# A graph-transformer layer: q and feed-forward matmuls ahead of the values in plain-block steps, two pairs of heads side by side

## The chip, the core and the metric

One core of one Trainium2 chip runs the whole program: TensorE (PE) for matmuls, VectorE (DVE), ScalarE (ACT) and GpSimd (POOL) for the rest, SyncE (SP) for issuing DMAs. The metric is device time of one execution in microseconds (us), and lower is better.

## The reference, cut to what matters

```
qkv = layer_norm(x, g1, be1) @ w_qkv            # x: 4096 x 128, 8 heads of 16
scores = einsum('nhd,mhd->hnm', q, k) * SCALE
scores = where(adj != 0, scores, -inf)          # adj: 4096 x 4096, int32
attn = softmax(scores, axis=-1)
out = einsum('hnm,mhd->nhd', attn, v).reshape(n, 128)
x = x + out @ w_proj + b_proj
h2 = layer_norm(x, g2, be2)
return x + gelu(h2 @ w1 + b1) @ w2 + b2         # hidden width 512
```

## The kernel before, in words

A prologue makes keys, values and masks for all 4096 rows. Then the queries go by in eight tiles of 512. A tile has 64 steps: four pairs of heads, 16 steps for each, and each step takes two blocks of 128 keys (`BLOCKS`). The code of an iteration `i` does tile `i` and also finishes tile `i - 1`; flags b, c, d say which of these parts exist (next tile to prepare, this tile, tile before). In the text, "step 23" is the iteration's step `g = 23`, and TensorE's instructions of step 23 are those that its loop `body` writes for that g. Behind tile 7 one more iteration, the drain, only finishes the last tile.

Each engine has an order that is written out by hand, and semaphores connect them. In one step:
- TensorE makes two row-score units into `ring_ps` (`row`, L960: scores with queries on the partitions, from which VectorE takes the masked row maximum, L763, for a pair that comes later), then the mask matmuls (L1112) and the score matmuls (L1127) of two blocks into `score_ps`, then two more row units, then the values: `weigh_values` (L1023) multiplies the probabilities of the step three steps back (`LAG`) by v and adds into `pv_ps`. Behind the values comes what the tables `ACT_FILLS` and `DVE_FILLS` give for the step.
- ScalarE takes the exponential of both blocks (L728), two of them in each step, then the fill of `ACT_FILLS`.
- VectorE takes four row maxima, then the fill of `DVE_FILLS`.
- GpSimd multiplies by the mask those blocks that have no mask matmuls ("plain" blocks, one in each odd step; `mask_probs`, L517), converts the adjacency for the next tile (L452, L456), splits maxima, adds q parts (L595), and does gelu's polynomial and gate (`bend`, `gate`) and the second layer norm's apply.

`score_ps` has two halves that are used in turn. `score_turn` makes TensorE wait, before it writes place n, until ScalarE has taken place n - 2. A fill of `ACT_FILLS` has a place of its own behind the two of its step, so it waits for the first exponential of its own step; the second block of the next step waits for ScalarE to have taken the fill. In an odd step the plain block comes first: its scores, then the masks and scores of the other block. In an even step both mask groups come first, then both scores; with a fill ahead, the second of these mask groups (x4 of the x8) is the one that waits.

Fills of `ACT_FILLS`: h2 transposed (`h2t`, steps 16, 17), the layer up (`up`, L1046, steps 19, 21, 23, 25; ScalarE takes it twice, L689 and L690), q of the next tile (`q`, L1036, steps 31, 34, 37, 41; ScalarE takes it twice, L675 and L676), and the shifts (`shift`, L927, two short copies L612 on ScalarE, steps 4, 14, 20, 30, 36, 46, 52, 62). Fills of `DVE_FILLS`: for each pair the softmax sums (`sums`, L1056) in the step four behind the pair's end and the way back of the reciprocals (`back`, L1062) one later, the projection of the tile before (`proj`, L1071, steps 6 and 7), the layer down (`down`, steps 30 to 33).

When a pair's 16 steps are through, `pv_ps` holds it in four groups of 32 rows: two heads, for each of the two blocks of a step. ScalarE copies it out in one piece (`take_values`, L701, 128x512) at the start of step 3, 19, 35 or 51, ahead of that step's exponentials. TensorE's values of that step start the next pair and wait for the copy. `sums` adds both parts of a head by a matmul with `sum_sel`, `back` spreads the reciprocals, VectorE multiplies (L863), and `proj` adds four pairs.

## Time and profile before

| | |
|---|---|
| runs | 1806.6, 1814.01 and 1814.49 us, median 1814.01 |
| the profiled execution | 1812.5 us, of which 1810.7 us are its span, 1.8 us lie around it |
| busy share | TensorE 92%, VectorE 78%, ScalarE 72%, GpSimd 65% |
| chain that ended last | TensorE 71%, ScalarE 15%, issue 10%, VectorE 2% |
| first and last copy of a pair (L701) | start at 180.1 and 1764.0 us |

The table is read against the span: a share of 92% for TensorE is an average over a short prologue, eight tiles that are alike and the drain. The chain says which engine the end hung on, step by step. What a change in one step is worth has to be read in that step, where TensorE and ScalarE take turns in waiting.

### The profile page before, as it was taken

Reading aid. Unit: us, or ns where it says so; the run is one execution under the profiler, and the core shown is the slowest. Engines: PE = TensorE matmul, PEld = TensorE weight load, DVE = VectorE, ACT = ScalarE, POOL = GpSimd, SP = SyncE. Lnnn points to the kernel's source line nnn. Section 1 sums busy time; section 2 is a strip of 40 time slices with the busy share of each in tenths; the row PEclk is TensorE's granted clock in tenths of the full one; section 3 lists DMA queues with packets and bytes.
Section 4 is the critical chain, followed back from the end, with each engine's and each line's share of the span. In section 5 each row is a group of like instructions: output and inputs, shape, how many; then the busy total and the mean of one; then the engine's idle time right before and its main releaser. Section 6 shows DMA issues by size and latency. Waiting matters only on the chain.

```text
span 1810.7 us, 48122 instructions
## 1 busy us (share of the span) xinstructions
PE 1673.6 (92%) x17826; PEld 553.9 (31%) x17826; DVE 1421.2 (78%) x4495; ACT 1300.8 (72%) x1443; POOL 1179.4 (65%) x1113
## 2 busy tenths in 40 slices
PE   6989999999999999999999999999999999999985
PEld 3422222323223232323223232323223232233223
DVE  6888889877898779887888779887898778987601
ACT  4547777677776777777776877677776877777771
POOL 5944586568855787468855688458865688457441
PEclk9869999999999999999999999999999999999996
DMA  7710035202450035301360035300351024500000
GB/s 214 168 42 2 25 108 110 54 1 66 135 100 2 13 106 117 66 1 54 114 133 2 1 100 124 77 2 26 123 106 47 2 77 124 77 2 1 8 7 6
DMA packets 168846, 115.24 MB, mean 64 GB/s; under 512 B 139298, under 2 KB 149156, under 8 KB 168612
## 3 DMA queue, kind: packets, MB, share of 16 engines
q1 hardware_dynamic: 157860, 103.78, 23.7%
q10 hardware_dynamic: 10752, 8.39, 1.6%
q8 instruction: 141, 2.31, 0.5%
q14 instruction: 93, 0.76, 0.1%
HBM read 74.39 MB, written 4.19 MB: 43 GB/s over the span
## 4 chain that ended last, share of the span: by engine, by line
PE 71%; ACT 15%; issue 10%; DVE 2%; DMA 1%; POOL 0%; SPq 0%; ACTq 0%; DVEq 0%; POOLq 0%
PE pv_ps L1023 19%; PE ring_ps L960 14%; PE score_ps L1127 12%; PE score_ps L1112 12%; ACT probs L728 12%; PE score_ps L1046 2%; PE ring_ps L1080 2%; PE ring_ps L1071 2%; PE ring_ps L1056 2%; PE ring_ps L1062 2%; PE score_ps L1036 2%; PE score_ps L984 2%; ACT q_stack L612 1%; ACT hidden L689 1%; DMA adj_in<-adj 1%
## 5 line engine op out<-in xcount | busy, mean ns | idle before, releaser
L763 DVE CUSTOM_DVE_ANT_0 masked_out<-ring_ps,row_mask 128x512 bf16<-128x512 f32 x2048 | 1310.3, 687 | 163.2 <-PE ring_ps L960 129.4
L728 ACT ACTIVATE probs<-score_ps,score_scale 128x1024 f32<-128x1024 f32 x1024 | 1089.0, 1113 | 358.0 <-PE score_ps L1127 350.4
L517 POOL TENSOR_TENSOR probs<-probs,keep 128x1024 int32<-128x1024 int32 x256 | 604.4, 2362 | 324.3 <-ACT probs L728 313.3
L1023 PE MATMUL pv_ps<-probs,v_ones 128*17 128x512 f32 x4096 | 539.2, 599 | 0.5 <-POOL probs L517 0.4
L960 PE MATMUL ring_ps<-k_stack,q_stack 51*64 51x512 f16 x4096 | 493.3, 397 | 13.3 <-DVE row_max L763 12.8
L1127 PE MATMUL score_ps<-q_stack,k_stack 51*64 51x512 f16 x4096 | 373.5, 391 | 26.6 <-ACT probs L728 7.4
L1112 PE MATMUL score_ps<-mask_t,ident_bf 64*64 64x512 bf16 x3072 | 276.1, 387 | 60.9 <-ACT probs L728 14.6
L960 PEld LDWEIGHTS ring_ps<-k_stack,q_stack 51*64 51x64 f16 x4096 | 165.8, 104 | 454.7 <-DVE row_max L763 401.9
L1127 PEld LDWEIGHTS score_ps<-q_stack,k_stack 51*64 51x64 f16 x4096 | 116.9, 104 | 229.2 <-PE score_ps L1112 181.1
L763 DVE DVE_READ_ACCUMULATOR2_ANT row_max<- 128x1 f32 x2048 | 169.4, 83 | 0.0
L1112 PEld LDWEIGHTS score_ps<-mask_t,ident_bf 64*64 64x64 bf16 x3072 | 92.4, 105 | 211.3 <-ACT probs L728 114.1
L456 POOL TENSOR_SCALAR row_mask<-row_mask 128x1024 bf16<-128x1024 bf16 x124 | 129.9, 1047 | 23.9 <-POOL row_mask L452 20.2
L452 POOL TENSOR_SCALAR row_mask<-adj_in 128x1024 bf16<-128x1024 uint32 x124 | 129.2, 1042 | 3.6 <-DVE row_max L763 1.7
L1023 PEld LDWEIGHTS pv_ps<-probs,v_ones 128*17 128x17 f32 x4096 | 68.1, 95 | 141.5 <-issue 110.1
L461 POOL TENSOR_SCALAR max_unit<-neg_max 128x4 f32<-128x4 f32 x64 | 12.7, 199 | 84.2 <-DVE neg_max L773 82.5
L860 DVE RECIPROCAL recip<-ring_ps 128x8 f32<-128x8 f32 x32 | 6.6, 208 | 77.5 <-PE ring_ps L1056 77.5
L612 ACT COPY q_stack<-score_ps 2x256 f16<-2x256 f16 x128 | 46.6, 364 | 9.5 <-PE score_ps L927 7.2
L876 DVE TENSOR_TENSOR rows<-ring_ps,x_res 128x128 f32<-128x128 f32 x32 | 9.3, 292 | 54.5 <-PE ring_ps L1080 54.5
L863 DVE TENSOR_TENSOR attn<-ring_ps,attn 128x512 f32<-128x512 f32 x32 | 22.1, 692 | 37.3 <-PE ring_ps L1062 37.3
L509 POOL TENSOR_SCALAR keep<-mask_t 128x512 int32<-128x512 bf16 x64 | 39.8, 622 | 5.4
L1046 PE MATMUL score_ps<-h2T,w_sb 128*128 128x512 f32 x64 | 39.8, 707 | 3.0 <-ACT hidden L693 2.3
L1080 PE MATMUL ring_ps<-w_sb,hidden 128*128 128x128 f32 x256 | 38.2, 295 | 2.0 <-DVE rows L876 1.1
(106 smaller groups left out, 969.6 us busy)
## 6 DMA issues: line engine op xcount, KB each, us to landing
adj_in<-adj SPq DMA_DIRECT2D x128, 512.0 KB, 4.1
xnT_dram<-attn ACTq DMA_DIRECT2D x8, 256.0 KB, 3.9
mask_t<-row_mask SPq DMA_TRANSPOSE x128, 3.4
xq<-xnT_dram ACTq DMA_DIRECT2D x8, 256.0 KB, 2.6
x_res<-x ACTq DMA_DIRECT2D x8, 256.0 KB, 4.4
out<-rows ACTq DMA_DIRECT2D x8, 256.0 KB, 2.6
w_sb<-L_gnn_w SPq DMA_DIRECT2D x2, 256.0 KB
probs<-x SPq DMA_DIRECT2D x1, 256.0 KB, 2.9
```

Source lines behind the costliest of these rows:

```text
L452: nc.gpsimd.tensor_scalar(target, adj_in[:, half, :].bitcast(U32), 1.0, 0.0, ALU.min, ALU.max)\
L456: nc.gpsimd.tensor_scalar(target, target, BIG, -BIG, ALU.mult, ALU.add).then_inc(mask_done, 1)
L517: nc.gpsimd.tensor_tensor(view, view, keep[:, KEPT.index(m), :].unsqueeze(1).broadcast_to([128, 2, TILE]), ALU.mult).then_inc(probs_masked, 1)
L612: last = nc.scalar.copy(stack[r:r + SHIFT_PARTS, p, 256 * jj:256 * (jj + 1)], bank.bitcast(F16)[r:r + SHIFT_PARTS, 0:256])
L728: nc.scalar.activation(probs[:, (2 * g + n) % SLOTS, :], score_ps[:, half:half + 2, :].rearrange("p a n -> p (a n)"), ACT.Exp, scale=score ...
L763: nc.vector.tensor_tensor_reduce(out=masked_out[:, place % 3, :], in0=ring_ps[:, place % 3, :], in1=row_mask[:, j, ch * 512:(ch + 1) * 512 ...
L960: last = nc.tensor.matmul(ring_ps[64 * t:64 * (t + 1), place % 3, :], stack[rows, p, first:first + 64], k_stack[rows, p, ch, K_FIRST:], st ...
L1023: last = nc.tensor.matmul(pv_ps[32 * k:32 * k + HD + 1, :], v_ones[:, block_of(g, b), 2 * p + a, :], probs[:, (2 * g + b) % SLOTS, a * TIL ...
L1046: last = nc.tensor.matmul(bank, w1_sb[:, 128 * f:128 * (f + 1)], h2T[:, :], start=True, stop=True)
L1080: last = nc.tensor.matmul(bank[:, 0:128], hidden[:, f, 128 * s:128 * (s + 1)], w2_sb[:, f, :], start=(f == 0), stop=(f == FC - 1))
L1112: last = nc.tensor.matmul(bank[to, :], ident_bf[keys, keys], mask_t[keys, source, :], start=True, stop=False)
L1127: last = nc.tensor.matmul(bank[64 * t:64 * (t + 1), :], k_stack[rows, p, m // 4, at + 64 * t:at + 64 * (t + 1)], q_stack[par][rows, p, :], ...
```

## The change

The fills of the odd steps of `ACT_FILLS` (h2t 1, the four `up`, the `q`) come ahead of the values on TensorE; the q of step 34 goes to step 35, so that all q stand in odd steps. ScalarE now copies a finished pair in two pieces of 64 rows into a new tile `halves`, on the partitions that its pair has there (even pair below, odd pair above). Behind every second pair GpSimd adds the two parts (`sum_values`, 128x512) into `attn`, in which two pairs now lie side by side, four heads in groups of 32 rows. So there are two `sums` and two ways back for a tile in place of four (steps 4 and 36), the way back of the tile before is split over steps 5 and 6, and the projection has half the matmuls and goes to steps 7 and 8. TensorE's values wait for the copy pieces (`values_taken`), its sums for GpSimd's add (`attn_ready`). The copy no longer waits for the projection. The projection's padded weights come by one small DMA less.

```diff
-ACT_FILLS = {16: ("h2t", 0), 17: ("h2t", 1), 31: ("q", 0), 34: ("q", 1), 37: ("q", 2), 41: ("q", 3)}
+ACT_FILLS = {16: ("h2t", 0), 17: ("h2t", 1), 31: ("q", 0), 35: ("q", 1), 37: ("q", 2), 41: ("q", 3)}
...
-DVE_FILLS = {4: ("sums", PAIRS - 1), 5: ("back", PAIRS - 1), 6: ("proj", 0), 7: ("proj", 1)}
+DVE_FILLS = {4: ("sums", FOURS - 1), 5: ("back", FOURS - 1, 0, 2), 6: ("back", FOURS - 1, 2, 4),
+             7: ("proj", 0), 8: ("proj", 1)}
...
-for _p in range(PAIRS - 1):
-    DVE_FILLS.update({QUARTER * (_p + 1) + 4: ("sums", _p), QUARTER * (_p + 1) + 5: ("back", _p)})
+DVE_FILLS.update({2 * QUARTER + 4: ("sums", 0), 2 * QUARTER + 5: ("back", 0, 0, SUB)})
...
+            def sum_values(n, f):
+
+                pool.wait_ge(values_taken, n)
+                settled(pool)
+                nc.gpsimd.tensor_tensor(attn[:, f, :], halves[:, 0, :], halves[:, 1, :], ALU.add).then_inc(attn_ready, 1)
...
+                    if d and g == LAG + 1:
+                        sum_values(i * PAIRS, FOURS - 1)
+                    if c and g == 2 * QUARTER + LAG + 1:
+                        sum_values(i * PAIRS + 2, 0)
...
-            def take_values(i, p, seen, proj):
+            def take_values(n, p, seen):
 
                 act.wait_ge(pv_done, seen)
-                if proj is not None:
-                    act.wait_ge(row_full, proj)
-                nc.scalar.copy(attn[:, p, :], pv_ps[:, :]).then_inc(attn_ready, 1)
+                if n >= 2:
+                    act.wait_ge(attn_ready, n // 2)
+                own = slice(64 * (p % 2), 64 * (p % 2 + 1))
+                nc.scalar.copy(halves[own, 0, :], pv_ps[0:64, :])
+                nc.scalar.copy(halves[own, 1, :], pv_ps[64:128, :]).then_inc(values_taken, 1)
...
-                    pe.wait_ge(attn_ready, i * PAIRS + p)
+                    pe.wait_ge(values_taken, i * PAIRS + p)
...
-                    for s in range(SUB):
+                    if what[2] == 0:
+                        pe.wait_ge(row_taken, made(ROWS, i, bcd, DVE_PLACE[g - 1]))
+                    for s in range(what[2], what[3]):
...
-                        for p in range(PAIRS):
-                            last = nc.tensor.matmul(bank[:, 128 * t:128 * (t + 1)], attn[:, p, 128 * s:128 * (s + 1)],
-                                                    wp_pad[:, p, :], start=(p == 0), stop=(p == PAIRS - 1))
+                        for f in range(FOURS):
+                            last = nc.tensor.matmul(bank[:, 128 * t:128 * (t + 1)], attn[:, f, 128 * s:128 * (s + 1)],
+                                                    wp_pad[:, f, :], start=(f == 0), stop=(f == FOURS - 1))
...
+                    if g in act_fills and g % 2 == 1:
+                        act_fill(i, bcd, g, act_fills[g])
                     if g < LAG and d:
                         weigh_values(i - 1, made_by(i - 1), STEPS - LAG + g)
                     if g >= LAG and c:
                         weigh_values(i, bcd, g - LAG)
-                    if g in act_fills:
+                    if g in act_fills and g % 2 == 0:
                         act_fill(i, bcd, g, act_fills[g])
```

TensorE in tile 3, step 23 and the start of step 24, before (`ring_ps` are rows, `mask_t` masks, `q_stack1,k_stack` into `score_ps` scores, `pv_ps` the values, `h2T,w1_sb` the layer up):

```order
L960 MATMUL ring_ps<-k_stack,q_stack1 64x512 x4
L1127 MATMUL score_ps<-q_stack1,k_stack 64x512 x4
L1112 MATMUL score_ps<-mask_t,ident_bf 64x512 x4
L1127 MATMUL score_ps<-q_stack1,k_stack 64x512 x4
L960 MATMUL ring_ps<-k_stack,q_stack1 64x512 x4
L1023 MATMUL pv_ps<-probs,v_ones 17x512 x4
L1046 MATMUL score_ps<-h2T,w1_sb 128x512
L960 MATMUL ring_ps<-k_stack,q_stack1 64x512 x4
L1112 MATMUL score_ps<-mask_t,ident_bf 64x512 x8
```

and after:

```order
L971 MATMUL ring_ps<-k_stack,q_stack1 64x512 x4
L1138 MATMUL score_ps<-q_stack1,k_stack 64x512 x4
L1123 MATMUL score_ps<-mask_t,ident_bf 64x512 x4
L1138 MATMUL score_ps<-q_stack1,k_stack 64x512 x4
L971 MATMUL ring_ps<-k_stack,q_stack1 64x512 x4
L1057 MATMUL score_ps<-h2T,w1_sb 128x512
L1034 MATMUL pv_ps<-probs,v_ones 17x512 x4
L971 MATMUL ring_ps<-k_stack,q_stack1 64x512 x4
L1123 MATMUL score_ps<-mask_t,ident_bf 64x512 x8
```

The layer up has moved ahead of the values; nothing else has.

TensorE in tile 3, from the values of step 5 to the fill of step 6 and the rows behind it, before (`ident,recip` the way back, `wp_pad,attn` the projection):

```order
L1023 MATMUL pv_ps<-probs,v_ones 17x512 x4
L1062 MATMUL ring_ps<-ident,recip 32x128 x16
L960 MATMUL ring_ps<-k_stack,q_stack1 64x512 x4
L1112 MATMUL score_ps<-mask_t,ident_bf 64x512 x8
L1127 MATMUL score_ps<-q_stack1,k_stack 64x512 x8
L960 MATMUL ring_ps<-k_stack,q_stack1 64x512 x4
L1023 MATMUL pv_ps<-probs,v_ones 17x512 x4
L1071 MATMUL ring_ps<-wp_pad,attn 128x128 x8
L960 MATMUL ring_ps<-k_stack,q_stack1 64x512 x4
```

and after:

```order
L1034 MATMUL pv_ps<-probs,v_ones 17x512 x4
L1074 MATMUL ring_ps<-ident,recip 32x128 x8
L971 MATMUL ring_ps<-k_stack,q_stack1 64x512 x4
L1123 MATMUL score_ps<-mask_t,ident_bf 64x512 x8
L1138 MATMUL score_ps<-q_stack1,k_stack 64x512 x8
L971 MATMUL ring_ps<-k_stack,q_stack1 64x512 x4
L1034 MATMUL pv_ps<-probs,v_ones 17x512 x4
L1074 MATMUL ring_ps<-ident,recip 32x128 x8
L971 MATMUL ring_ps<-k_stack,q_stack1 64x512 x4
```

The way back stands in two pieces of 8, the second where the first projection was; that one now stands in step 7, with 4 matmuls for 8.

ScalarE in tile 3 around the copy of step 35, before (`q_neg` and `q_x` are the two takes of a q fill):

```order
L675 ACTIVATE q_neg<-score_ps,part_coef 128x512
L676 COPY q_x<-score_ps 128x512
L739 DMA out<-rows2 128x4x128
L701 COPY attn<-pv_ps 128x512
L728 ACTIVATE probs<-score_ps,score_scale 128x1024 x4
L612 COPY q_stack1<-score_ps 2x256 x2
L728 ACTIVATE probs<-score_ps,score_scale 128x1024 x2
L675 ACTIVATE q_neg<-score_ps,part_coef 128x512
```

and after:

```order
L738 ACTIVATE probs<-score_ps,score_scale 128x1024 x6
L749 DMA out<-rows2 128x4x128
L713 COPY halves<-pv_ps 64x512
L714 COPY halves<-pv_ps 64x512
L738 ACTIVATE probs<-score_ps,score_scale 128x1024 x2
L686 ACTIVATE q_neg<-score_ps,part_coef 128x512
L687 COPY q_x<-score_ps 128x512
L738 ACTIVATE probs<-score_ps,score_scale 128x1024 x2
```

The copy is two pieces, and the take of the second q has gone from ahead of the copy to behind the exponentials of step 35.

## Rows read from the trace of the kernel before

**Rows 1.** The page: span, and busy time of each engine.

```profile
span 1810.7 us, 48122 instructions
...
PE 1673.6 (92%) x17826; PEld 553.9 (31%) x17826; DVE 1421.2 (78%) x4495; ACT 1300.8 (72%) x1443; POOL 1179.4 (65%) x1113
```

**Rows 2.** One line, the copy of a finished pair: shortest/median/longest, first and last start.

```profile
L701 ACT COPY attn<-pv_ps x32: 584/586/599, 180.1 to 1764.0; 128x512 f32<-128x512 f32 x32
```

**Rows 3.** Timeline of TensorE, tile 3, steps 22 to 24: start, us, instruction [idle before].

```profile
807.38 0.63 PE L1127 MATMUL score_ps<-q_stack,k_stack 51*64 51x512 f16 x8
...
811.16 1.05 PE L1023 MATMUL pv_ps<-probs,v_ones 128*17 128x512 f32 x8
812.14 1.12 PE L1046 MATMUL score_ps<-h2T,w_sb 128*128 128x512 f32 x2
...
814.63 0.41 PE L1112 MATMUL score_ps<-mask_t,ident_bf 64*64 64x512 bf16 x4 [0.80 <-ACT q_x L690]
814.87 0.65 PE L1127 MATMUL score_ps<-q_stack,k_stack 51*64 51x512 f16 x8
```

**Rows 4.** Timeline of ScalarE over the same steps.

```profile
807.90 2.12 ACT L728 ACTIVATE probs<-score_ps,score_scale 128x1024 f32<-128x1024 f32 x2 [0.35 <-PE score_ps L1127]
810.22 2.12 ACT L728 ACTIVATE probs<-score_ps,score_scale 128x1024 f32<-128x1024 f32 x2 [0.20 <-PE score_ps L1127]
813.31 0.69 ACT L689 ACTIVATE hidden<-score_ps,b_col 128x512 f32<-128x512 f32 x1 [0.96 <-PE score_ps L1046]
813.89 0.68 ACT L690 ACTIVATE q_x<-score_ps,b_col 128x512 f32<-128x512 f32 x1
```

**Rows 5.** Timeline of ScalarE, steps 34 and 35: exponentials, the copy of a pair.

```profile
849.68 2.12 ACT L728 ACTIVATE probs<-score_ps,score_scale 128x1024 f32<-128x1024 f32 x2 [2.12 <-PE score_ps L1127]
...
853.33 0.60 ACT L701 COPY attn<-pv_ps 128x512 f32<-128x512 f32 x1
853.81 2.14 ACT L728 ACTIVATE probs<-score_ps,score_scale 128x1024 f32<-128x1024 f32 x2
```

**Rows 6.** A group of short copies: busy us, mean ns, idle before.

```profile
L612 ACT COPY q_stack<-score_ps 2x256 f16<-2x256 f16 x128 | 46.6, 364 | 9.5 <-PE score_ps L927 7.2
```

**Rows 7.** Timeline of TensorE, tile 3, steps 52 and 53.

```profile
907.66 1.05 PE L1056 MATMUL ring_ps<-sum_sel,attn 128*128 128x2 f32 x8
...
909.10 0.39 PE L1112 MATMUL score_ps<-mask_t,ident_bf 64*64 64x512 bf16 x4
...
911.19 1.06 PE L1062 MATMUL ring_ps<-ident,recip 128*32 128x128 f32 x32
```

**Rows 8.** Timeline of ScalarE, step 52.

```profile
908.27 0.74 ACT L612 COPY q_stack<-score_ps 2x256 f16<-2x256 f16 x2
```

**Rows 9.** Timeline of TensorE, step 6: a projection.

```profile
753.89 2.05 PE L1071 MATMUL ring_ps<-wp_pad,attn 128*128 128x128 f32 x16
```

**Rows 10.** Timeline of TensorE, steps 31, 36 and 42.

```profile
838.00 1.05 PE L1023 MATMUL pv_ps<-probs,v_ones 128*17 128x512 f32 x8
...
856.25 0.64 PE L1127 MATMUL score_ps<-q_stack,k_stack 51*64 51x512 f16 x8
...
877.29 0.41 PE L1112 MATMUL score_ps<-mask_t,ident_bf 64*64 64x512 bf16 x4 [0.69 <-ACT q_x L676]
```

**Rows 11.** Timeline of ScalarE, step 31.

```profile
837.07 2.12 ACT L728 ACTIVATE probs<-score_ps,score_scale 128x1024 f32<-128x1024 f32 x2 [0.47 <-PE score_ps L1127]
```

**Rows 12.** Timeline of GpSimd, tile 3, the masks of step 25 and what precedes them.

```profile
822.19 0.62 POOL L526 TENSOR_SCALAR rows<-rows 128x512 f32<-128x512 f32 x1 [0.97 <-ACT rows L690]
822.99 1.27 POOL L529 TENSOR_TENSOR rows<-rows,hidden 128x512 f32<-128x512 f32 x1 [0.18 <-POOL rows L526]
...
826.27 2.37 POOL L517 TENSOR_TENSOR probs<-probs,keep 128x1024 int32<-128x1024 int32 x1
```

**Rows 13.** Timeline of TensorE, step 28.

```profile
828.71 1.05 PE L1023 MATMUL pv_ps<-probs,v_ones 128*17 128x512 f32 x8
```

**Rows 14.** Timeline of TensorE, the drain behind tile 7.

```profile
1768.36 3.75 PE L1071 MATMUL ring_ps<-wp_pad,attn 128*128 128x128 f32 x16 [0.88 <-DVE attn L863]
```

More of the change, by code:

```diff
@@ L32 @@
 PAIRS = HEADS // 2
+FOURS = PAIRS // 2
 HALF = 64
@@ L96, in made_for @@
         return "b"
-    if what[0] == "shift" or (what[0] in ("sums", "back") and what[1] < PAIRS - 1):
+    if what[0] == "shift" or (what[0] in ("sums", "back") and what[1] < FOURS - 1):
         return "c"
@@ L277, in program @@
         max_part = sb("max_part", [128, 2, 4, SHIFT_PARTS], F16)
-        attn = sb("attn", [128, PAIRS, TILE], F32)
-        recip = sb("recip", [128, SUB, 2], F32)
+        attn = sb("attn", [128, FOURS, TILE], F32)
+        halves = sb("halves", [128, BLOCKS, TILE], F32)
+        recip = sb("recip", [128, SUB, 4], F32)
         x_res = sb("x_res", [128, SUB, DIM], F32)
@@ L298, in program @@
         xn_rows = [rows2[:, :, :], x_res[:, :, :]]
-        xnT = [attn[:, p, :] for p in range(4)]
+        xnT = [attn[:, 0, :], attn[:, 1, :], halves[:, 0, :], halves[:, 1, :]]
         item_neg = [hidden[:, n // 2, 256 * (n % 2):256 * (n % 2) + 256].bitcast(F16) for n in range(DEPTH)]
@@ L859, in take_fill @@
                 if what[0] == "sums":
-                    nc.vector.reciprocal(recip[:, :, :], bank[:, 0:2 * SUB].rearrange("p (s a) -> p s a", a=2))\
+                    nc.vector.reciprocal(recip[:, :, :], bank[:, 0:4 * SUB].rearrange("p (s k) -> p s k", k=4))\
                       .then_inc(row_taken, 1)
                 elif what[0] == "back":
-                    nc.vector.tensor_tensor(attn[:, what[1], :], bank, attn[:, what[1], :], ALU.mult)\
+                    own = slice(128 * what[2], 128 * what[3])
+                    nc.vector.tensor_tensor(attn[:, what[1], own], bank[:, own], attn[:, what[1], own], ALU.mult)\
                       .then_inc(row_taken, 1)
@@ L1158, in constants @@
 def constants():
-    c = np.zeros((128, 134), np.float32)
+    c = np.zeros((128, 136), np.float32)
     c[:, 0:128] = np.eye(128)
-    for a in range(2):
-        for b in range(BLOCKS):
-            c[64 * b + 32 * a + HD, 128 + a] = 1.0
+    for k in range(4):
+        c[32 * k + HD, 128 + k] = 1.0
     for r in range(128):
```

47 lines of the change are left out of this document (20 added, 27 removed).

## Prediction

> **What bounds the kernel now.** I read the page first. TensorE is busy for 92% of the span and the next engine, VectorE, for 78% [rows 1]. That alone says only that TensorE matters. The first and the last copy of a pair lie 1583.9 us apart with 31 pairs between them, so a pair takes 51.1 us and a step 3.19 us [rows 2]. The timelines of tile 3 then show who waits for whom in a step. There are two kinds of stretch. Where both a TensorE fill and more TensorE work stand in a step, TensorE runs without a gap, and what it no longer does is saved in full. Where ScalarE has a fill to take, TensorE waits for it: in step 24 its second mask group starts at 814.63 behind 0.80 us of idle time, released by ScalarE's second take of the layer up [rows 3]. That take began at 813.31, and ScalarE had been idle for 0.96 us before it, waiting for the layer-up matmul [rows 4]. So in such a pair of steps both engines wait once, one behind the other. The reader should see that loop: scores at 807.38, exponentials, values at 811.16, layer up at 812.14, take until 814.57 (813.89 + 0.68), masks, scores of step 24 at 814.87, which makes 7.49 us.
>
> **The projection (-2.0 us per tile that has one behind it).** A projection fill is 2.05 us of TensorE [rows 9] and there are two for a tile. Half the matmuls go, 2 x 1.0. The steps were TensorE's alone, so this is on the path. The way back of the old tile is the same 16 matmuls in two halves and costs what it did. VectorE gets two multiplies of half the width for one.
>
> **Sums and ways back of the pairs that no longer have their own (-2.0).** Steps 20 and 52 lose their sums, steps 21 and 53 their way back. The sums look like 1.05 us [rows 7], but in those steps ScalarE copies a shift. In step 52 it does so from 908.27 to 909.01 [rows 8], and TensorE's masks of step 53 start at 909.10 [rows 7]: they would wait for the shift copies with or without the sums. I take 0 for the sums; the cover is the shift, and without it each would be worth another 1.0. The ways back have no such cover behind them: 1.06 us each [rows 7], 2 x 1.0.
>
> **Fills ahead of the values (-1.7 in all).** A fill must wait until the first exponential of its own step is over. In step 23 the exponentials start at 810.22 and two take 2.12 us [rows 4], so the first ends near 811.3, 0.1 behind the place where the values start today. The layer up can thus start some 0.8 us earlier than at 812.14, and up to 0.98 us where VectorE no longer delays the rows by a multiply. ScalarE takes it that much earlier, the 0.80 us wait of the masks goes, and values plus rows fill the gap. I take -0.9 for steps 23 and 25, -1.8. In step 21 today's way back already fills the wait, so the -1.0 above is all that this step gives, and it needs the early fill. The q of step 41 is alone like step 23: TensorE waits 0.69 us for its take [rows 10], -0.7. In steps 31 and 37 TensorE is not waiting for ScalarE: there the early fill only meets the exponential. In step 31 that starts at 837.07 [rows 11] and its first half ends near 838.15, while TensorE is ready at 838.00 [rows 10]: +0.2 each. In step 35 it is worse. ScalarE is through with step 34 at 851.80 (849.68 + 2.12), then come two copies at 0.48 each (853.33 to 853.81) and one exponential of 1.1 [rows 5], so the q fill can start at 853.85 only; with 1.1 for it (its 1.12 overlap a little with what follows), 0.98 for the values (811.16 to 812.14) and three groups of four matmuls at 0.24 (814.63 to 814.87 [rows 3]) the scores of step 36 come at 856.65 and not at 856.25 [rows 10]: +0.4, the gain of having no q in step 34 included. Step 19 has copies too, and its gain of 0.8 is eaten by the second copy and the wait behind it: 0. The h2 transposes of step 17 are short: 0. Sum: -1.8 - 0.7 + 0.2 + 0.2 + 0.4 = -1.7.
>
> **The second copy (+0.8).** The trace has no copy of 64 rows from 512 columns. Below, half the rows could take half the time, 0.3 us each, and the pair of copies would cost nothing; above, each takes the full 0.586 us [rows 2]. The shift copies have 2 rows and 256 columns and still take 0.364 us [rows 6], which is far over a sixty-fourth, so rows are not what ScalarE pays for: I take the upper end, +0.48 from start to start. The Trainium skill's page "ScalarE: Activation LUTs" (Rules for kernel authors) speaks against this part of the change: it budgets some 0.3 us for each ACTIVATE and 0.83 ns per element. Read per partition that is 0.72 us for each piece; by that rule the 64 pieces would cost at most 9 us more than I count. The trace's 0.586 us is shorter, and I keep it. The copies stand ahead of the exponentials; behind them wait the masks of the next step. In steps 3 and 51 TensorE is just in time today, so about +0.4 each. Those of steps 19 and 35 are in the term above. TensorE's values of the same step, with the next rows queued behind them, now wait for both pieces; they stand behind the first mask group and one set of scores and rows, which hides the 0.48. The copy no longer waits for a projection that was over many steps before: 0.
>
> **GpSimd's add (0 in the tiles).** 128x512 in float32 takes 1.27 us there [rows 12], twice for a tile. What is queued behind it are the masked probabilities of steps 3 and 35, which TensorE's values want three steps later, over 9 us at 3.19 us a step; that hides it. The sums wait for it. In step 36 the copies end near 852.7, a conversion may be ahead on GpSimd, and TensorE is at the scores of step 36 at 856.65, with values still before the sums: more than a microsecond to spare. If that cover is gone, it costs up to 1.3 us for a tile.
>
> **Sum.** Tiles 1 to 6: -2.0 - 2.0 - 1.7 + 0.8 = -4.9 each, -29.4. Tile 0 has neither projection nor layer up: -2.0, -0.7, +0.8 for steps 31, 35 and 37, +0.8 for copies: -1.1. Tile 7 has no q: -2.0 - 2.0 - 1.8 + 0.4 + 0.8 = -4.6. In the drain nothing overlaps: a projection fill takes 3.75 us [rows 14], two halves less is -3.75; a copy +0.5 and the add +1.4 in full: -1.9. Total -37.0. The profiled execution took 1812.5 us, so 1775.5; the median of the runs shown is 1.5 us above it. I predict 1775.
>
> **Rivals.**
> - *The copies are cheap and all of TensorE's saving shows.* Then +0.8 goes, step 35 costs nothing and step 19 gains like step 23: -1.9 more a tile, 15 in all: 1760. For it: TensorE's 92%. Against: the 0.364 us of the 2-row copy.
> - *GpSimd's chain holds the layer-up steps.* Polynomial, gate and mask form a chain there: from 822.19 to 828.64 (826.27 + 2.37), 6.45 us for two steps [rows 12], and TensorE's values of step 28, which need that mask, start at 828.71 [rows 13], 0.07 us later. Two steps would now take 6.5 us. The chain starts when ScalarE has taken the layer up, and so moves with it, but there is no slack. If it slips, the 1.8 and one way back are lost, 2.8 x 7: 1795.
> - *The sums wait for GpSimd's add,* 1.3 x 8: 1786. Against it: the spare microsecond above.
> - *Slower: early fills hold TensorE.* Every early fill stands ahead of the values on an engine that runs in order. If ScalarE, with the copies on top, stays an exponential late, each of nine fills costs 0.9 us and gains nothing: +8.1 instead of -1.7, so +4.9 for a tile, 34 in all: 1846. It turns to a loss where the mean fill costs over 0.35 us. Against it: ScalarE had 0.96 us of idle time before the take in step 23, and only step 35 reaches such a price.
> - *Nothing changes,* since another wait takes over everywhere: near 1812. VectorE, the next engine, has 22% idle time.
>
> **How the numbers follow.** My forecast 0.60 (1767 to 1784); cheap copies 0.14; GpSimd's chain 0.12; waiting sums 0.05; early fills slower 0.06; nothing 0.03. The range from 1758 to 1795 holds all but the last two and some edges. A measurement of this kernel tells 0.5% from no change, 9 us: faster 0.90, same 0.04, slower 0.06.
>
> **What would show it.** The two pieces of the copy near 0.59 us each (half that: the first rival). The pair of steps 22 and 23 in 6.5 us rather than 7.49, with the 0.80 us wait before the masks of step 24 gone. Projection fills of 1.05 us. Step 52 as long as before, step 53 1.0 us shorter. TensorE idle before the q of step 35 by nearly 1 us. TensorE's values of step 28 waiting for GpSimd would say that the second rival holds; sums with GpSimd as releaser, the third. The prediction is wrong if the distance between first copies of successive tiles shrinks by less than 3 or more than 7 us.

## The result and the profile after

The changed kernel takes 1792.65 us (median of 6 runs, 1792.28 to 1798.58) against 1813.3 us for the kernel before (6 runs): the ratio is 0.9889, with an interval from 0.9873 to 0.9906. The prediction took 37 us off the profiled execution; the profiled executions differ by 19.9 (1812.5 and 1792.59 us). The page of the new one:

```profile
span 1790.8 us, 46610 instructions
...
PE 1640.1 (92%) x17058; PEld 516.3 (29%) x17058; DVE 1411.1 (79%) x4471; ACT 1322.5 (74%) x1475; POOL 1198.3 (67%) x1129
```

TensorE is busy 33.5 us less and still for 92% of a shorter span [rows 1]. To read where the time went I took the start of TensorE's first values matmul in each step (L1034 now, L1023 before); what a step takes is the distance from its values to those of the next step. The 64 distances of a tile are compared as a mean over tiles 1 to 6. A tile took 207.70 us and takes 204.62: -3.08, where -4.9 was forecast.

| part of a tile | predicted | measured |
|---|---|---|
| steps 5 to 8, projection | -2.0 | -2.13 |
| steps 18 to 21, way back, early fills and copies | -1.0 | -1.12 |
| steps 52 and 53, sums and way back | -1.0 | -1.09 |
| steps 22 to 26, two layers up | -1.8 | -1.42 |
| steps 40 to 42, q | -0.7 | -0.66 |
| steps 2, 3 and 51, second copy | +0.8 | +1.06 |
| steps 16 and 17, 30 and 31, 36 and 37 | +0.4 | +0.64 |
| steps 34 and 35, q in a copy step | +0.4 | +1.44 |
| all others | 0 | +0.20 |

Outside of these tiles: tile 0 +0.6 (predicted -1.1), tile 7 -3.0 (-4.6), and from the start of the last values to the end +1.0 (-1.9).

The groups of ScalarE's short copies: busy us, mean ns of one, idle before; the first line answers to [rows 6], the other two to [rows 2].

```profile
L623 ACT COPY q_stack<-score_ps 2x256 f16<-2x256 f16 x128 | 46.6, 364 | 9.5 <-PE score_ps L938 7.2
...
L714 ACT COPY halves<-pv_ps 64x512 f32<-64x512 f32 x32 | 18.6, 582 | 0.4
L713 ACT COPY halves<-pv_ps 64x512 f32<-64x512 f32 x32 | 18.3, 573 | 3.1 <-PE pv_ps L1034 2.7
```

A piece of 64 rows takes 573 or 582 ns, as long as the 586 ns of all 128 rows.

TensorE's timeline in tile 3 from the scores of step 22 to those of step 24, which answers to [rows 3]:

```profile
798.88 0.63 PE L1138 MATMUL score_ps<-q_stack,k_stack 51*64 51x512 f16 x8
...
802.75 1.13 PE L1057 MATMUL score_ps<-h2T,w_sb 128*128 128x512 f32 x2
803.81 1.05 PE L1034 MATMUL pv_ps<-probs,v_ones 128*17 128x512 f32 x8
...
805.03 0.62 PE L1123 MATMUL score_ps<-mask_t,ident_bf 64*64 64x512 bf16 x8
805.50 0.63 PE L1138 MATMUL score_ps<-q_stack,k_stack 51*64 51x512 f16 x8
```

and ScalarE's, which answers to [rows 4]:

```profile
799.40 4.31 ACT L738 ACTIVATE probs<-score_ps,score_scale 128x1024 f32<-128x1024 f32 x4 [0.32 <-PE score_ps L1138]
803.92 0.69 ACT L700 ACTIVATE hidden<-score_ps,b_col 128x512 f32<-128x512 f32 x1 [0.21 <-PE score_ps L1057]
804.50 0.68 ACT L701 ACTIVATE q_x<-score_ps,b_col 128x512 f32<-128x512 f32 x1
805.07 0.63 ACT L746 ACTIVATE rows<-rows 128x512 f32<-128x512 f32 x1
806.02 4.30 ACT L738 ACTIVATE probs<-score_ps,score_scale 128x1024 f32<-128x1024 f32 x4 [0.32 <-PE score_ps L1138]
```

The scores (L1138) of the two steps are 6.62 us apart (805.50 - 798.88), and were 7.49 [rows 3]. The layer up stands ahead of the values now; its take begins after 0.21 us of idle time and not 0.96 [rows 4], and the 0.80 us in front of TensorE's masks are gone. ScalarE is now idle for 0.53 us (0.21 + 0.32) of these 6.62: it is nearly full itself.

The way back in two pieces and the projection, TensorE's timeline of tile 3, which answers to [rows 9] and to the last line of [rows 7]:

```profile
744.39 0.62 PE L1074 MATMUL ring_ps<-ident,recip 128*32 128x128 f32 x16
...
747.50 0.62 PE L1074 MATMUL ring_ps<-ident,recip 128*32 128x128 f32 x16
...
750.72 1.16 PE L1082 MATMUL ring_ps<-wp_pad,attn 128*128 128x128 f32 x8
...
754.47 1.16 PE L1082 MATMUL ring_ps<-wp_pad,attn 128*128 128x128 f32 x8
```

A projection fill takes 1.16 us, and took 2.05 before [rows 9].

Now the place that went wrong. ScalarE in tile 1, the end of step 34 and step 35, which answers to [rows 5]:

```profile
432.39 1.11 ACT L738 ACTIVATE probs<-score_ps,score_scale 128x1024 f32<-128x1024 f32 x1
433.52 0.58 ACT L713 COPY halves<-pv_ps 64x512 f32<-64x512 f32 x1
434.11 0.58 ACT L714 COPY halves<-pv_ps 64x512 f32<-64x512 f32 x1
434.71 2.12 ACT L738 ACTIVATE probs<-score_ps,score_scale 128x1024 f32<-128x1024 f32 x2
437.04 0.69 ACT L686 ACTIVATE q_neg<-score_ps,part_coef 128x512 f16<-128x512 f32 x1 [0.20 <-PE score_ps L1047]
```

TensorE there (rows, the q fill, the values, the scores of step 36):

```profile
434.27 0.45 PE L971 MATMUL ring_ps<-k_stack,q_stack 51*64 51x512 f16 x4
435.88 1.12 PE L1047 MATMUL score_ps<-xq,wq_rep 128*128 128x512 f32 x2 [1.15 <-ACT probs L738]
436.93 1.05 PE L1034 MATMUL pv_ps<-probs,v_ones 128*17 128x512 f32 x8
...
438.62 0.63 PE L1138 MATMUL score_ps<-q_stack,k_stack 51*64 51x512 f16 x8
```

From the start of the first copy to the start of the exponentials ScalarE needs 1.19 us (434.71 - 433.52), 0.6 for each piece; before, one copy took 0.48 (853.81 - 853.33) [rows 5]. TensorE has the q fill next in its order and stands idle for 1.15 us in front of it, with the values ready behind it. In this tile steps 34 and 35 take 5.11 + 2.67 = 7.78 us, 0.71 more than before (4.40 + 2.67). In tiles 2, 3 and 5 they take 9.15, 9.29 and 9.25. The same stretch of 5 us around this q fill in tiles 0 to 6, busy times and granted clock (PEclk):

```profile
core 0: us, PE busy (x) PEld busy (x) DVE busy (x) ACT busy (x) POOL busy (x), PEclk, DMA share, GB/s
229.50:234.50 5.00, 3.77 (x18) 0.78 (x18) 1.52 (x6) 3.38 (x5) 4.70 (x5) 0.66 0.48 165
434.60:439.60 5.00, 3.85 (x38) 1.05 (x34) 2.64 (x9) 3.83 (x6) 4.70 (x5) 1.00 0.49 154
638.10:643.10 5.00, 3.84 (x22) 0.82 (x22) 1.60 (x6) 3.41 (x5) 4.70 (x5) 0.72 0.49 155
843.20:848.20 5.00, 3.85 (x18) 0.64 (x18) 1.56 (x6) 3.37 (x5) 4.41 (x5) 0.69 0.45 156
1049.20:1054.20 5.00, 3.85 (x38) 1.05 (x34) 2.64 (x9) 3.82 (x6) 4.70 (x5) 1.00 0.50 155
1252.70:1257.70 5.00, 3.85 (x18) 0.64 (x18) 1.63 (x6) 3.44 (x5) 4.70 (x5) 0.70 0.47 156
1458.70:1463.70 5.00, 3.85 (x38) 1.05 (x34) 2.65 (x9) 3.82 (x6) 4.70 (x5) 1.00 0.50 159
```

In tiles 0, 2, 3 and 5 the granted clock is 0.66 to 0.72 over the stretch, which means that a part of it runs at 1.2 and not at 2.4 GHz; in tiles 1, 4 and 6 it is 1.00. In tile 3 the q fill then takes 1.55 us, and 1.12 in tile 1, and the values 1.91 and 1.05. What TensorE did before is the same in all seven: it was idle for 1.15 us (1.23 in tile 0). The loss is 1.4 us and more each time. In its profiled execution the kernel before shows no half clock in its tiles; TensorE's idle times there are 0.8 us at most, but for one of 1.04 at the end of tile 7.

The drain, TensorE's timeline, which answers to [rows 14]:

```profile
1745.81 1.52 PE L1067 MATMUL ring_ps<-sum_sel,attn 128*128 128x4 f32 x8 [2.82 <-POOL attn L581]
1747.77 1.08 PE L1074 MATMUL ring_ps<-ident,recip 128*32 128x128 f32 x16 [0.44 <-DVE recip L870]
1749.39 1.08 PE L1074 MATMUL ring_ps<-ident,recip 128*32 128x128 f32 x16 [0.54 <-DVE attn L874]
1751.02 2.08 PE L1082 MATMUL ring_ps<-wp_pad,attn 128*128 128x128 f32 x8 [0.55 <-DVE attn L874]
```

and GpSimd's add ahead of the sums:

```profile
1744.41 1.26 POOL L581 TENSOR_TENSOR attn<-halves 128x512 f32<-128x512 f32 x1 [2.52 <-ACT halves L714]
```

and TensorE before:

```profile
1764.68 1.02 PE L1056 MATMUL ring_ps<-sum_sel,attn 128*128 128x2 f32 x8 [0.80 <-ACT attn L701]
1766.10 1.38 PE L1062 MATMUL ring_ps<-ident,recip 128*32 128x128 f32 x32 [0.39 <-DVE recip L860]
...
1772.63 3.78 PE L1071 MATMUL ring_ps<-wp_pad,attn 128*128 128x128 f32 x16 [0.52 <-DVE x_res L869]
```

The two projection fills end 4.67 us after the first begins; before, 8.05. That is -3.4. Against it stand the second copy (+0.6), the add (1.26 us and the handing over on both sides, +1.4), the sums, which end at half clock (1.52 for 1.02, +0.5), and the way back. From its start to the projection's it takes 3.25 us (1751.02 - 1747.77) and took 2.26 (1768.36 - 1766.10), +1.0. The waits for VectorE in it are only 0.2 us more (0.54 + 0.55 for 0.88); TensorE itself is busy 0.8 us longer, with two pieces of 1.08 us for one of 1.38. Most of that is the clock: in experiment 10 the first of these pieces fell ahead of the half clock and took 0.64 us. So the projection ends 13.75 us after the last values begin and not earlier than before (13.58). Of the layer down before, the last two of four pieces took 1.16 us each at the full clock; now all four take 1.70 us or more, 9.04 us for 7.54 in all. With the norm and the layer up between them 0.7 us shorter, that is the +1.0 (0.2 + 1.5 - 0.7).

### The profile page after: what moved, and what is told of

Its sections match the earlier page's. It is cut to its first block, busy times and chain, and to the rows that moved or that the text cites. A ratio compares the mean times of both kernels' runs of the same rounds, so it can differ in the third digit from the quotient of the medians.

```text
span 1790.8 us, 46610 instructions
## 1 busy us (share of the span) xinstructions
PE 1640.1 (92%) x17058; PEld 516.3 (29%) x17058; DVE 1411.1 (79%) x4471; ACT 1322.5 (74%) x1475; POOL 1198.3 (67%) x1129
## 4 chain that ended last, share of the span: by engine, by line
PE 61%; ACT 22%; issue 12%; DVE 2%; DMA 1%; POOL 1%; ACTq 0%; SPq 0%; DVEq 0%; POOLq 0%
ACT probs L738 19%; PE pv_ps L1034 17%; PE ring_ps L971 11%; PE score_ps L1123 11%; PE score_ps L1138 10%; PE score_ps L1057 2%; PE ring_ps L1091 2%; PE score_ps L1047 2%; ACT q_stack L623 2%; PE score_ps L995 2%; PE ring_ps L1082 1%; PE ring_ps L1067 1%; PE ring_ps L1074 1%; ACT halves L714 1%; DVE masked_out L773 1%
## 5 line engine op out<-in xcount | busy, mean ns | idle before, releaser
L1034 PE MATMUL pv_ps<-probs,v_ones 128*17 128x512 f32 x4096 | 542.4, 602 | 1.8 <-POOL probs L518 0.4
L1138 PE MATMUL score_ps<-q_stack,k_stack 51*64 51x512 f16 x4096 | 372.0, 391 | 32.2 <-ACT probs L738 13.0
L1138 PEld LDWEIGHTS score_ps<-q_stack,k_stack 51*64 51x64 f16 x4096 | 116.6, 104 | 243.5 <-PE score_ps L1123 181.8
L1034 PEld LDWEIGHTS pv_ps<-probs,v_ones 128*17 128x17 f32 x4096 | 68.7, 95 | 169.4 <-issue 100.2
L870 DVE RECIPROCAL recip<-ring_ps 128x16 f32<-128x16 f32 x16 | 4.1, 258 | 72.8 <-PE ring_ps L1067 72.8
L1047 PE MATMUL score_ps<-xq,wq_rep 128*128 128x512 f32 x56 | 33.4, 679 | 10.7 <-ACT probs L738 10.2
```

Source lines behind the costliest of these rows:

```text
L1034: last = nc.tensor.matmul(pv_ps[32 * k:32 * k + HD + 1, :], v_ones[:, block_of(g, b), 2 * p + a, :], probs[:, (2 * g + b) % SLOTS, a * TIL ...
L1138: last = nc.tensor.matmul(bank[64 * t:64 * (t + 1), :], k_stack[rows, p, m // 4, at + 64 * t:at + 64 * (t + 1)], q_stack[par][rows, p, :], ...
```

## The experiments

The kernel before, run beside them, took 1811.43 us with experiments 1 to 4, 1812.99 with 5 to 8 (one run each) and 1814.13 with 9 and 10. The time of a single run also has in it how often the clock fell, so experiments 5 to 8 are read by their steps.

**1. The order alone (k1_order_only).** The kernel before with only the odd fills ahead of the values; q stays in 34, copies and sums as before.

```diff
+                    if g in act_fills and g % 2 == 1:
+                        act_fill(i, bcd, g, act_fills[g])
...
-                    if g in act_fills:
+                    if g in act_fills and g % 2 == 0:
```

> The kernel before with one part of the change: in odd steps the fill of ScalarE's table stands ahead of the values; nothing else (q stays in steps 31, 34, 37, 41, one copy of 128 rows, four sums). If the early fills are worth what the trace of the change shows in the layer-up steps (steps 22 to 25 went from 14.8 to 13.2 us), this alone takes -0.8 each in steps 19, 23 and 25 and -0.7 in step 41, gives back 0.2 to 0.4 in steps 31 and 37: about -2.5 us per tile, 17 us in all, near 1796. If the early fills are what failed to pay in the change, it stays within 5 us of the kernel before.

Measured: 1801.83 us (1799.24 to 1803.88), ratio 0.9939 (0.9922 to 0.9956), -1.69 a tile: -0.53 in steps 18 and 19, -1.48 in 22 to 26, -0.66 in 40 to 42, and +0.13, +0.42 and +0.36 in 16/17, 30/31 and 36/37 (the last with a fall of the clock in one tile; without it, 0.1). Early fills pay 0.5 to 0.7 us each where TensorE waited for ScalarE, and cost up to 0.4 where it did not. I had expected 1796: with the fall of the clock left out a tile gains 2.0 us and not 2.5, and step 21, where the way back stays, gains nothing.

**2. The pairs side by side alone (k2_fours_only).** The changed kernel with every fill behind the values and q in step 34.

```diff
-ACT_FILLS = {16: ("h2t", 0), 17: ("h2t", 1), 31: ("q", 0), 35: ("q", 1), 37: ("q", 2), 41: ("q", 3)}
+ACT_FILLS = {16: ("h2t", 0), 17: ("h2t", 1), 31: ("q", 0), 34: ("q", 1), 37: ("q", 2), 41: ("q", 3)}
...
-                    if g in act_fills and g % 2 == 1:
-                        act_fill(i, bcd, g, act_fills[g])
...
-                    if g in act_fills and g % 2 == 0:
+                    if g in act_fills:
```

> The change without its order: every fill stands behind the values and the second q is back in step 34; two copies, GpSimd's add, two sums and halved projection stay. Projection -2.0, ways back of 21 and 53 at most -2.0 per tile; but in step 21 the wait for ScalarE's take of the layer up comes back (+0.8), and each of four double copies costs what the trace of the change shows in steps 2 to 3 and 51, 0.5 to 0.6 (2.2 in all): -1.0 per tile, and +1.0 in the drain: near 1807. If both parts are additive, the savings of this and of the order alone sum to the 20 us of the change; if the change lost something where the parts meet (a q behind two copies in step 35), they sum to more than 20.

Measured: 1802.58 us (1799.21 to 1804.79), ratio 0.9942 (0.9924 to 0.9961), -1.42 a tile. The sum -1.69 - 1.42 = -3.11 is close to the -3.08 of the whole, but that is chance. The clock fell in three of tiles 1 to 6 of the changed kernel, in one of experiment 1 and in none here; without these falls it is -1.96 - 1.42 = -3.4 against -3.8. The two parts help each other a little, in steps 20 to 26: the early fill of step 21 pays only where the way back is gone, as the prediction had it. The result is 4 us better than I had expected. The saving on TensorE and the price of the copies are both in this number: steps 5 to 8 give 2.1, steps 52 and 53 give 1.1, and steps 2/3, 34/35 and 51 take back 0.62, 0.67 and 0.44.

**3. q back in step 34 (k3_q_34).** The changed kernel, only the table.

```diff
-ACT_FILLS = {16: ("h2t", 0), 17: ("h2t", 1), 31: ("q", 0), 35: ("q", 1), 37: ("q", 2), 41: ("q", 3)}
+ACT_FILLS = {16: ("h2t", 0), 17: ("h2t", 1), 31: ("q", 0), 34: ("q", 1), 37: ("q", 2), 41: ("q", 3)}
```

> The change with the second q back in step 34, behind the values. Theory one: the shortfall against the forecast sits mostly where a q is both early and behind two copies: TensorE idles 1.15 us ahead of it and in tiles 0, 2, 3 and 5 its granted clock is then at half for 3.4 us. Then steps 34 and 35 together take 7.07 us plus about 0.7 for the copies, not 8.5, no half clock shows in any tile, and the kernel takes 5 to 7 us less than the change, near 1786. Theory two: the copies cost the same wherever the q stands: steps 34 and 35 stay within 0.2 us of the change's 8.5 in the undisturbed tiles (7.8 there), and only the 4 clock drops of 1.2 us go: 1788.

Measured: 1787.72 us (1786.06 to 1790.39), ratio 0.9859 (0.9841 to 0.9877). Steps 34 to 37 take 4.65 + 3.09 + 5.05 + 3.68 = 16.47 us at the full clock, and 16.51 in the changed kernel. So the place of the fill itself is worth nothing at the full clock; what can differ is the clock. My first theory had no half clock in any tile, and that was wrong: it shows in two tiles here (4 and 6, from step 36 on), where the changed kernel had it in four. On 34 and 35 the two theories do not differ (7.74 us, as both had it), and the interval of this kernel's time just touches that of the changed one. TensorE in tile 4:

```profile
1054.59 1.74 PE L1047 MATMUL score_ps<-xq,wq_rep 128*128 128x512 f32 x2 [0.16 <-ACT probs L738]
1056.25 1.91 PE L1034 MATMUL pv_ps<-probs,v_ones 128*17 128x512 f32 x8
```

This is the early q fill of step 37, behind a wait of 0.16 us; the largest wait in the 8 us before it is 0.44 us.

**4. q in 31, 37, 39, 41 (k4_q_39).** No fill near the copies of step 35.

```diff
-ACT_FILLS = {16: ("h2t", 0), 17: ("h2t", 1), 31: ("q", 0), 35: ("q", 1), 37: ("q", 2), 41: ("q", 3)}
+ACT_FILLS = {16: ("h2t", 0), 17: ("h2t", 1), 31: ("q", 0), 37: ("q", 1), 39: ("q", 2), 41: ("q", 3)}
```

> The change with q in steps 31, 37, 39, 41, so that no q shares a step with a copy and all are early. Theory one: steps 34 and 35 take 2.8 + 3.1 us (as steps 50 and 51 of the change) and the q in step 39 costs 1.2 us as the one in step 41 does: 1.4 to 1.6 us less per tile than the change, 10 to 11 us in all, near 1782. If q and copy did not hurt each other, only the position of a stall moves and the time stays within 3 us of the change.

Measured: 1786.84 us (1782.86 to 1791.54), ratio 0.9858 (0.9834 to 0.9883), -3.68 a tile. Steps 34 and 35 fall to 3.00 + 3.09, while step 38 rises by 1.28. At the full clock steps 34 to 38 take 0.4 us less than in the changed kernel, so of the 1.4 to 1.6 us that I had expected for a tile the rest would be the clock's, and it fell again. The same loss turned up at the other copy step that has an early fill, step 19, in two tiles. TensorE in tile 4, the layer up of step 19 and the values behind it:

```profile
985.66 1.64 PE L1057 MATMUL score_ps<-h2T,w_sb 128*128 128x512 f32 x2 [1.01 <-ACT probs L738]
987.23 1.91 PE L1034 MATMUL pv_ps<-probs,v_ones 128*17 128x512 f32 x8
```

Here too the clock fell after TensorE had been idle (1.01 us) in front of an early fill behind two copies. But the same 1.01 us stand in step 19 of the other five such tiles of this run, and of all seven of the changed kernel, and there it did not fall.

**5. q of step 35 behind its values (k5_q35_late).**

```diff
-                    if g in act_fills and g % 2 == 1:
+                    if g in act_fills and g % 2 == 1 and g != 35:
...
-                    if g in act_fills and g % 2 == 0:
+                    if g in act_fills and (g % 2 == 0 or g == 35):
```

> The change with one fill moved: the q of step 35 stands behind the values of that step; every other early fill stays. Theory one (the early place is what hurts in step 35): TensorE no longer idles 1.15 us in one piece ahead of the q but 0.3 there and some more ahead of the masks of step 36, so its granted clock does not fall in step 35 of any tile. Theory two (the copies are what hurts): steps 34 to 37 together take within 0.3 us of what the change needs where its clock did not fall (16.5 us), and about 1.4 us less than in the tiles where it fell.

Measured: 1784.91 us in one run, beside 1812.99 for the kernel before. TensorE in tile 3, values, q, and the second mask group of step 36:

```profile
842.46 1.05 PE L1034 MATMUL pv_ps<-probs,v_ones 128*17 128x512 f32 x8
843.51 1.12 PE L1047 MATMUL score_ps<-xq,wq_rep 128*128 128x512 f32 x2
...
845.89 0.41 PE L1123 MATMUL score_ps<-mask_t,ident_bf 64*64 64x512 bf16 x4 [0.70 <-ACT q_x L687]
```

The idle stretch is 0.70 us, behind the q fill and not in front of it, and steps 34 to 37 take 16.20 us in every one of tiles 1 to 6, with no fall of the clock in them. It fell once in this run, in step 19 of tile 3, behind the 1.01 us wait of experiment 4. That one line is worth 0.3 us a tile at the full clock, and the falls in step 35 on top. Not all of the difference to the changed kernel is the edit's: 2.5 us of it lie in the drain, which the edit does not touch. The early placement that gains in step 23 loses in step 35.

**6. The copy in two pieces of 64 rows (k6_copy_rows).** The kernel before, only this.

```diff
-                nc.scalar.copy(attn[:, p, :], pv_ps[:, :]).then_inc(attn_ready, 1)
+                nc.scalar.copy(attn[0:64, p, :], pv_ps[0:64, :])
+                nc.scalar.copy(attn[64:128, p, :], pv_ps[64:128, :]).then_inc(attn_ready, 1)
```

> The kernel before with the copy of a pair in two pieces of 64 rows, each to the same rows (no shift of partitions), nothing else. If half the rows are as dear as all, and such an instruction does not overlap its neighbours on ScalarE (as the shift copies of 2 rows already do not), the pieces last 0.59 us each, lie 0.59 us apart, and the exponentials start 1.2 us behind the end of those before, where one copy needs 0.47: +0.6 us in each of the four steps with a copy, 15 to 20 us in all, near 1830. If rows were what is paid for, each piece lasts 0.3 us and the kernel stays at 1812.

Measured: 1824.13 us in one run, beside 1812.99; each piece keeps its rows here, so no shift of partitions is in it. ScalarE in tile 3, step 3:

```profile
745.61 0.57 ACT L701 COPY attn<-pv_ps 64x512 f32<-64x512 f32 x1
746.19 0.58 ACT L702 COPY attn<-pv_ps 64x512 f32<-64x512 f32 x1
746.79 2.12 ACT L729 ACTIVATE probs<-score_ps,score_scale 128x1024 f32<-128x1024 f32 x2
```

**7. The copy in two pieces of 256 columns (k7_copy_columns).** The same number of elements in each piece, but on all 128 rows.

```diff
-                nc.scalar.copy(attn[:, p, :], pv_ps[:, :]).then_inc(attn_ready, 1)
+                nc.scalar.copy(attn[:, p, 0:256], pv_ps[:, 0:256])
+                nc.scalar.copy(attn[:, p, 256:512], pv_ps[:, 256:512]).then_inc(attn_ready, 1)
```

> The kernel before with the copy in two pieces of 128 rows and 256 columns. If the columns are what is paid for, with a fixed part, a piece lasts near 0.36 us (the shift copies: 2 rows, 256 columns, 0.364 us). If instructions over all 128 rows overlap by 0.1 us and those over part of them do not, the pieces are 0.25 us apart and the pair costs 0.5 us, no more than one copy: the time stays within 3 us of before. If it is the number of instructions that costs, whatever their rows, the pair costs 0.7 us or more.

Measured: 1813.73 us in one run, beside 1812.99. ScalarE in tile 3, step 3:

```profile
742.46 0.37 ACT L701 COPY attn<-pv_ps 128x256 f32<-128x256 f32 x1
742.71 0.39 ACT L702 COPY attn<-pv_ps 128x256 f32<-128x256 f32 x1
742.98 2.15 ACT L729 ACTIVATE probs<-score_ps,score_scale 128x1024 f32<-128x1024 f32 x2
```

By rows the two pieces hold ScalarE for 1.18 us (746.79 - 745.61), and each begins when the one before it has ended. By columns they hold it for 0.52 us, and each begins 0.12 us before the end of the one ahead, like the undivided copy, which holds it for 0.48. Dividing by rows cost 0.49 us in steps 2 and 3, 0.53 in 34 and 35, 0.44 in 51, and in 18 and 19 only 0.12; dividing by columns cost no step over 0.03 in the mean. So what the second copy costs is not that there are two instructions, but that each has half the rows: the full time of its columns, and no overlap. Columns are no substitute in this change, which needs each piece of rows on other partitions.

**8. The last add on VectorE (k8_drain_add).** In the drain alone.

```diff
-                    if d and g == LAG + 1:
+                    if d and c and g == LAG + 1:
...
+                if not c:
+                    dve.wait_ge(values_taken, i * PAIRS)
+                    settled(dve)
+                    nc.vector.tensor_tensor(attn[:, FOURS - 1, :], halves[:, 0, :], halves[:, 1, :], ALU.add)\
+                      .then_inc(attn_ready, 1)
```

> The change with the add of the last two pairs on VectorE in the drain alone (all adds inside the tiles stay on GpSimd). In the drain nothing lies beside the add: GpSimd takes 1.27 us and its wait 0.2 more. On VectorE some 0.7 us: the drain gets 0.6 to 0.9 us shorter. TensorE is idle 2.8 us there between the last values and the sums, and its granted clock is at half for the 41 us from there on, where it was at half for 10 us, at full for 3 and at half for 24 before; if this idle time is what brings that, 2.1 us of it may not, and the down matmuls go back from 9.0 to 7.5 us.

Measured: 1791.18 us in one run, and 47.0 us from the last values to the end where the changed kernel has 48.9. TensorE's sums in the drain:

```profile
1745.64 1.02 PE L1072 MATMUL ring_ps<-sum_sel,attn 128*128 128x4 f32 x8 [2.22 <-DVE attn L917]
```

They begin 3.27 us after the last values and not 3.87, and take 1.02 us at the full clock. 0.6 us is the add's; the rest of the 1.9 is the clock's: sums 0.5 and the layer down 0.7 (8.34 us and not 9.06). That last is no result of the edit, for in experiments 2 to 5, whose drains are the same as the changed kernel's, the layer down takes anything from 7.3 to 9.4 us.

**9. The layer up a pair of steps later (k12_up_21).** No fill in the copy step 19; the layer down and the store come one step later too.

```diff
-UP_STEPS = [19 + 2 * f for f in range(FC)]
+UP_STEPS = [21 + 2 * f for f in range(FC)]
...
-DVE_FILLS.update({30 + s: ("down", s) for s in range(SUB)})
+DVE_FILLS.update({31 + s: ("down", s) for s in range(SUB)})
...
-STORE_STEP = 34
+STORE_STEP = 35
...
```

> The changed kernel with the four layer-up fills a pair of steps later (21, 23, 25, 27, so that none stands in the copy step 19), and the layer down with its last rows one step later. Theory: what a pair of steps costs is ScalarE's work in it, an early fill needs a pair without copies. Then steps 18 and 19 fall from about 7.9 to 6.1 us (as steps 34 and 35 with no q in them) and steps 26 and 27 rise from 5.5 to 6.6: -0.6 us a tile, 1788 us. Rival, GpSimd's chain of polynomial, gate and mask binds the layer-up steps: moved closer to the masks of step 27 and later it would show as TensorE's values of steps 28 and 30 waiting for GpSimd, 1 us or more a tile, 1800 us.

Measured: 1783.03 us (1778.98 to 1785.69), ratio 0.9825 (0.9808 to 0.9843). Steps 18 and 19 take 2.86 + 3.09 = 5.95 us (7.64 in the changed kernel), steps 26 and 27 take 6.62 (5.50), and steps 18 to 30 together give 0.58 against the changed kernel, as the theory had it for a tile. The time is 5 us better than the 1788 expected, and part of that is the clock, which in the profiled execution fell in two tiles (2 and 3, from step 36 on) and not in four. The rival is in it, small: in step 29 TensorE waits for GpSimd's masks.

```profile
822.86 1.05 PE L1034 MATMUL pv_ps<-probs,v_ones 128*17 128x512 f32 x8 [0.72 <-POOL probs L518]
```

**10. All together (k11_best).** The layer up in 21 to 27, q in 33, 37, 39, 41, h2t 1 behind the values, the layer down a step later, the last add on VectorE. Against the changed kernel:

```diff
-UP_STEPS = [19 + 2 * f for f in range(FC)]
-ACT_FILLS = {16: ("h2t", 0), 17: ("h2t", 1), 31: ("q", 0), 35: ("q", 1), 37: ("q", 2), 41: ("q", 3)}
+UP_STEPS = [21 + 2 * f for f in range(FC)]
+ACT_FILLS = {16: ("h2t", 0), 17: ("h2t", 1), 33: ("q", 0), 37: ("q", 1), 39: ("q", 2), 41: ("q", 3)}
...
-                    if g in act_fills and g % 2 == 1:
+                    if g in act_fills and g % 2 == 1 and g != 17:
...
```

> The changed kernel with what the runs so far say: q in steps 33, 37, 39, 41 and the layer up in 21, 23, 25, 27 (no fill in a copy step), h2t 1 behind the values again, the layer down one step later, and in the drain the last add on VectorE. Theory, the parts add: the run with q in 31, 37, 39, 41 took 1786.8 us; less 0.6 a tile for the layer up, 0.13 a tile for h2t, 1.9 for the drain's add makes 1779. Rival, the gains of q and of layer up overlap, since ScalarE is the bound of all of these pairs and its work only moves: 1786 us, as without them.

Measured: 1781.49 us (1779.8 to 1782.7), ratio 0.9819 (0.9806 to 0.9833), -4.28 a tile, and no tile shows a fall of the clock. It is the fastest kernel here, 11 us under the changed one, but not told apart from experiment 9, whose interval overlaps. Against experiment 4 the rival was right inside the tiles: where no tile of either shows a fall of the clock they take nearly the same, 203.0 to 203.5 us here and 203.1 to 203.8 there (tiles 1 to 3 and 6). Steps 18 to 20 gain 1.4 us and steps 30 to 32 0.8. Step 26, ahead of the last layer up, gives back 1.1, step 29 0.7, where the wait for GpSimd is as in experiment 9, and steps 34 and 35 0.3, where the layer down now meets the end of the q pair. The rest is the clock, which fell in two tiles of experiment 4 (1.6 us each) and in none here, and the drain: from the last values to the end 45.8 us for 47.6.

## Why the prediction was right, and where its sizes were off

The signs inside the tiles and the waits came out as forecast, and the time lies in the stated range. But 1792.65 us is outside the 1767 to 1784 that I gave 0.60, and close to the 1795 of the rival with GpSimd's chain, which did not happen. The test of the first copies of successive tiles (less than 3 us would be wrong) was passed with 3.0 and nothing to spare. That the number held owes something to the width of the range.

**The projection, -2.0: right.** -2.13, and the same in every run that has it.

**Sums at nothing because the shift copies hide them, ways back at 1.0 each: right.** Step 52 lost its sums and changed by -0.07; step 53 lost its way back and changed by -1.02.

**Early fills, -1.7: right in its mechanism, too large.** Experiment 1 isolates it. The layer-up pairs gained 0.5 to 0.9 us, since at 6.62 us ScalarE has 0.53 us of idle time left and sets their length. I had taken TensorE's wait as the gain and not asked what ScalarE's own work in the pair adds up to. Steps 31 and 37 cost 0.42 and 0.1 for 0.2 each, and h2t 1 cost 0.13 for 0.

**Step 35, +0.4: the term that failed.** +0.71 at the full clock: 1.19 us for the two copies, where the sum had 2 x 0.48, gives 0.23 of the missing 0.3. And then the clock, which the prediction did not have as a term at all. The sum itself said that TensorE would be idle by nearly 1 us before this fill; it was 1.15 us, in four of seven tiles the clock fell at it, and each fall cost 1.4 to 1.8 us: about 6 of the 17 us between forecast and result. In experiment 5, with q behind the values, the idle time is shorter, the step costs the same in every tile, and no fall stands there.

That the clock falls because of the idle stretch is not shown. The profiled executions of all twelve kernels have 17 falls in their tiles: 7 at the 1.15 us wait of step 35 (14 such waits, in the changed kernel and in experiment 8), 3 at the 1.01 us wait of step 19 (35 such waits), 6 at the early q fill of step 37 behind waits of 0.16 us (experiments 1, 3, 8 and 9), and one in experiment 6, near no early fill. Experiment 8 has the changed kernel's tiles word for word, and there it fell in tiles 0, 1, 3 and 6 and not in 0, 2, 3 and 5. So the order of the instructions does not decide it alone. What can be said is that 16 of the 17 began within 1 us of the start of an early fill, that a wait of 1.15 us ahead of it had the most of them, and that the kernel before and experiments 2 and 7, with no early fill, had none; nor had experiment 10, whose early fills stand in no copy step. What decides stays open. The Trainium skill's page "TensorE: Matmul & The Clock Gate" (HAM oscillation — how this bites in real kernels) tells of a kernel whose long waits for a DMA put TensorE back to the slow clock in each turn of its loop. The waits here are far shorter, and six falls have hardly any wait before them, so that case does not explain these.

**The second copy, +0.8: right side, a little more.** +1.06. The upper end of the bound, one full time for each piece, was still too low by the overlap: start to start a piece takes 0.59 us and not 0.48. The Trainium skill's page "ScalarE: Activation LUTs" (What ACT_TABLE_LOAD costs) gives an overlap of about 93 ns for ACTIVATEs back to back. The whole copy [rows 5] and the pieces by columns come near it, at some 0.12 us; the pieces of 64 rows have none. The first rival, cheap copies, is out by experiment 6: dividing alone makes a tile of the kernel before 1.9 us longer, 0.3 of them one fall of the clock.

**GpSimd's add, 0 in the tiles: right.** In tile 3 the sums of step 36 came without a wait. The rival with GpSimd's chain did not come about in the changed kernel, and in experiments 9 and 10 it did, at 0.75 us in most tiles.

**The drain, -1.9: wrong sign, +1.0.** Projection, copy and add came as priced (-3.4, +0.6, +1.4). Missing was TensorE's clock in the drain, which the sum did not have as a term: it stands in the sums (+0.5), in most of the +1.0 of the way back (the waits for VectorE in its two pieces are 0.2 of it), and in 1.5 us of the layer down. The last is not the change's own: from run to run the layer down took 7.3 to 9.4 us in like drains. The norm and the layer up were 0.7 us shorter.

**The sum.** Of the 17.1 us between -37.0 and -19.9, tiles 1 to 6 make 10.9 (6 x 1.8; the clock in three of them 4.4), tile 0 1.7 (the clock there), tile 7 1.6 and the drain 2.9. The range held it.

## What to carry to other kernels

A fill may go ahead of other work on an in-order engine only where what it waits for is over by then. Add up the other engine's whole work in that step first: the same edit gained 0.7 us a step where ScalarE had exponentials alone and lost 0.3 where it had two copies on top, and a plan that leaves TensorE idle for 1 us ahead of such a fill may be paid for twice: half of the waits of 1.15 us here had a fall of the clock with them. Count a ScalarE copy that is cut along the partitions as a whole one for each piece, without overlap; if it must be cut and the place of the rows is free, cut its columns. And price the end of the program by itself, since what a pipeline hides (an extra add, a second copy) stands there in full, and TensorE's clock can be lower there.
